# Expert results added onto token rows by GpSimd's scatter, with five result tiles, and the first expert's weights and rows loaded earlier

## The reference

```python
xn = layernorm(x)
s = attn_ref(xn, ...)         # linear attention, 16 heads, a grouped convolution over 5 rows, an MLP of 1024 with gelu
g = silu(ffn_ref(xn, ...))
return x + s * g

# ffn_ref: a small causal attention over the 4 rows of one position, then 16 experts, two for each token
ln2 = layernorm(hidden_after_attn).reshape(-1, 256)           # T = 8192 tokens
probs = softmax(ln2 @ router_weight.T)
top_p, top_i = top_k(probs, 2)
cap = 1280                                                    # slots of an expert
keep = pos < cap                                              # pos: place of the token in its expert
buf = zeros((16, cap + 1, 256)).at[exp_idx, pos_c].add(ln2[tok] * keep[:, None])
h1 = gelu(einsum('ech,efh->ecf', buf, moe_w1))                # 256 -> 512
h2 = einsum('ecf,ehf->ech', h1, moe_w2)                       # 512 -> 256
out_ent = h2[exp_idx, pos_c] * (gate * keep)[:, None]
moe_out = zeros((T, 256)).at[tok].add(out_ent)
return hidden_after_attn + moe_out
```

## Time and profile before

| | us |
|---|---|
| median of 3 runs | 2015.42 |
| lowest, highest | 2011.74, 2019.06 |
| the profiled execution | 2010.27 |
| its span, first to last instruction | 2008.5 |
| PE busy | 1806.9 (90%) |
| DVE busy | 1382.0 (69%) |
| POOL busy | 968.5 (48%) |
| ACT busy | 818.0 (41%) |

### The profile page before, as it was taken

How to read it: one execution, slowest core, us unless ns; L and a number is a source line. 1 busy time by engine, 2 the same in 40 slices (tenths; PEclk the granted TensorE clock), 3 DMA queues, 4 the chain that set the end, 5 groups by cost and what they waited for, 6 DMA issues and landing times. The chain is left out here.

```text
span 2008.5 us, 37232 instructions
## 1 busy us (share of the span) xinstructions
PE 1806.9 (90%) x12775; PEld 1616.4 (80%) x12776; DVE 1382.0 (69%) x3571; ACT 818.0 (41%) x1945; POOL 968.5 (48%) x1502
## 2 busy tenths in 40 slices
PE   3999996398999999996999999999888899999998
PEld 2676775285998858996999999999875799875998
DVE  3988885754565535653777778877567588795786
ACT  2566663262332652331333333333355333472433
POOL 3666653565555665553556656566332233340431
PEclk7999997699999999997999999999989999999999
DMA  7555522024333233333334343242136021361121
GB/s 207 160 176 177 177 93 71 27 81 129 134 126 120 71 103 112 122 123 106 112 94 127 110 134 121 92 124 71 51 121 181 22 78 58 111 192 48 53 71 59
DMA packets 181942, 218.29 MB, mean 109 GB/s; under 512 B 22874, under 2 KB 165411, under 8 KB 181774
## 3 DMA queue, kind: packets, MB, share of 16 engines
q1 hardware_dynamic: 159006, 166.61, 26.7%
q0 software_dynamic: 18464, 49.49, 7.0%
q10 hardware_dynamic: 4304, 0.02, 0.1%
HBM read 114.94 MB, written 107.22 MB: 111 GB/s over the span
## 5 line engine op out<-in xcount | busy, mean ns | idle before, releaser
L1869 POOL DMA_INDIRECT picked_d<-h,home x160 | 163.6, 1022 | 192.3 <-DVE h L1916 156.7
L1795 ACT ACTIVATE hid<-bank 128x512 f32<-128x512 f32 x160 | 95.6, 597 | 335.6 <-PE bank L130 335.6
L128 PE MATMUL bank<-rows_hi,up_hi 128*128 128x256 f32 x640 | 189.1, 295 | 11.1 <-POOL up_lo L1863 7.1
L130 PE MATMUL bank<-rows_hi,up_lo 128*128 128x256 f32 x640 | 182.5, 285 | 0.0
L129 PE MATMUL bank<-rows_lo,up_hi 128*128 128x256 f32 x640 | 182.4, 285 | 0.0
L128 PE MATMUL bank<-down_hi,hid_hi 128*128 128x256 f32 x640 | 181.2, 283 | 0.0
L130 PE MATMUL bank<-down_hi,hid_lo 128*128 128x256 f32 x640 | 181.2, 283 | 0.0
L129 PE MATMUL bank<-down_lo,hid_hi 128*128 128x256 f32 x640 | 181.1, 283 | 0.0
L1199 POOL DMA_INDIRECT buf_d<-lt,to_row x128 | 134.6, 1052 | 85.3 <-POOL lt L1195 40.7
L1498 PE MATMUL bank<-wconv,knt 128*128 128x128 f32 x1280 | 157.2, 279 | 0.0
L1930 DVE TENSOR_TENSOR hid_lo<-hid,hid_hi 128x512 fp32r<-128x512 f32 x160 | 118.8, 752 | 52.2 <-ACT hid_hi L1795 49.4
(11 more groups left out here) (318 smaller groups left out, 5587.4 us busy)
## 6 DMA issues: line engine op xcount, KB each, us to landing
buf_d<-zeros SPq DMA_DIRECT2D x16, 1360.0 KB, 7.4
rows_in<-buf_d SPq DMA_DIRECT2D x80, 272.0 KB, 2.8
lt<-ln_d SPq DMA_DIRECT2D x128, 128.0 KB, 2.2
picked_d<-nothing SPq DMA_DIRECT2D x32, 512.0 KB, 3.2
job_picked<-picked_d SPq DMA_DIRECT2D x64, 256.0 KB, 2.9
x<-in_x SPq DMA_DIRECT2D x16, 512.0 KB, 4.1
after_d<-after SPq DMA_DIRECT2D x16, 512.0 KB, 2.9
ln_d<-ln SPq DMA_DIRECT2D x16, 512.0 KB, 2.9
```

What stands on the lines that cost most here:

```text
L128: pe.matmul(dst, hi, mhi, start=start and i == 0, stop=False)
L130: mm = pe.matmul(dst, lo, mhi, start=False, stop=end)
L1795: act.activation(dst[:, 2 * half:2 * half + 2].rearrange("p f c -> p (f c)"), bank[half][:], ACT.Gelu_apprx_tanh).then_inc(e_hid, 1)
L1869: pool.indirect_dma_start(picked_d, bass.IndirectOffsetOnAxis(home[i % TAG_RING][:, r:r + 1], axis=0), h2[p][:, r], None, bounds_check=PIC ...
```

## The change

1. `send` adds: the scatter has `compute_op=ALU.add` and goes to the token's row in `after_d`, so that after the experts this row holds `hidden_after_attn` plus both expert results. The home row of both slots is the token's number (the pattern of the iota changes from `[T, 2]` to `[0, 2]`). Two experts may add to the same row, so at the first chunk of each expert POOL waits until all earlier scatters have landed. `picked_d`, its clears, `nothing`, `mix` and the load of `job_after` are gone; a job's load of `after_d` goes straight to `picked[:, 0]`, and ACT's `silu` waits for that DMA.
2. `H2_RING` goes from 3 to 5, `TAG_RING` from 6 to 9, the jobs' `RING` from 3 to 4.
3. The buffers `up_w0`, `down_w0` and `rows_in` are allocated ahead of attention A, `lt` are the first two `rows_in`. POOL asks for expert 0's weights at the start of attention A. SP asks for the first three chunks of rows at the end of attention A, after the scatters have landed.
4. Expert 0's up weights are split by ACT (high) and DVE (low), its down weights by POOL.
5. In attention B, SP asks for the fourth group of x ahead of the first job's store, and DVE does the join ahead of `stats_x`.

```diff
-PICKED = 2 * T
-        picked_d = nc.dram_tensor("picked_d", (PICKED, E), F32).ap()
-                    pool.iota(tags[:, :, :, 1], pattern=[[P, TILES], [T, 2]], base=0, channel_multiplier=1,
+                    pool.iota(tags[:, :, :, 1], pattern=[[P, TILES], [0, 2]], base=0, channel_multiplier=1,
...
-        SCATTERS, RING = TILES // 2, 3
+        SCATTERS, RING = TILES // 2, 4
+        ROWS_AHEAD, H2_RING, TAG_RING = 3, 5, 9
+        early = ExitStack()
+        up_w0, down_w0 = sb("up_w0", [P, HALVES, FFN], into=early), sb("down_w0", [P, FC, E], into=early)
+        rows_in = [sb(f"rows_in{p}", [P, 2, ROW], into=early) for p in range(ROWS_AHEAD)]
+        def load_first_weights(pool):
+            pool.dma_start(up_w0[:], a["w1_t"][0].rearrange("(j p) f -> p j f", p=P)).then_inc(weights_in[0], 16)
+            pool.dma_start(down_w0[:], a["w2_t"][0].rearrange("(j p) f -> p j f", p=P)).then_inc(weights_in[0], 16)
...
-                            sp.dma_start(picked[p][:], picked_d.rearrange("(k t p) e -> p t k e", k=2, p=P)[:, t]).then_inc(job_in[p], 16)
-                            sp.dma_start(job_after[p][:], tile(after_d, t)).then_inc(job_in[p], 16)
+                            sp.dma_start(picked[p][:, 0], tile(after_d, t)).then_inc(job_in[p], 16)
...
-                                    if 1 <= i <= CLEARS // 2:
-                                        clear_picked((b - first) * CLEARS // 2 + i - 1)
                             for q in scattered:
                                 sp.wait_ge(q, 32 * EACH)
+                            for i in range(ROWS_AHEAD):
+                                sp.dma_start(rows_in[i][:], chunk_of(buf_d, i)).then_inc(rows_loaded[i], 16)
                             for q in s_out:
                                 sp.wait_ge(q, 16 * BT)
-                            sp.wait_ge(picked_clear, 16 * CLEARS)
...
                             load_x(first, 2)
+                            load_x(first, 3)
                             for job in range(2 * EACH):
                                 store_job(job)
...
-                                if job == 0:
-                                    load_x(first, 3)
...
+                        if scatters:
+                            load_first_weights(pool)
                         flow(opening, first_loop, middle, second_loop)
...
-                            act.wait_ge(job_mixed, job + 1)
+                            act.wait_ge(job_in[job % RING], 16 * (rounds(job) + s_loads(job)))
...
-                        def mix(job):
-                            p = job % RING
-                            rows = picked[p]
-                            dve.wait_ge(job_in[p], 32 * rounds(job))
-                            dve.tensor_tensor(rows[:, 0], rows[:, 0], rows[:, 1], ALU.add).then_inc(mix_step, 1)
-                            dve.wait_ge(mix_step, job + 1)
-                            dve.tensor_tensor(rows[:, 0], rows[:, 0], job_after[p][:], ALU.add).then_inc(job_mixed, 1)
...
+                    act.wait_ge(weights_in[0], 32)
+                    act.activation(up_s[0][0][:], up_w[0][:], ACT.Copy).then_inc(first_up, 1)
...
                         if i % CHUNKS == 0:
-                            pe.wait_ge(weights_split, 4 * x + 2)
+                            if x == 0:
+                                pe.wait_ge(first_up, 2)
+                            else:
+                                pe.wait_ge(weights_split, SPLITS(x, 2))
...
                     def send(i):
                         p = i % H2_RING
                         pool.wait_ge(h2_made, i + 1)
+                        if i and i % CHUNKS == 0:
+                            for q in range(H2_RING):
+                                pool.wait_ge(h2_out[q], 32 * len(range(q, i, H2_RING)))
                         for r in range(2):
-                            pool.indirect_dma_start(picked_d, bass.IndirectOffsetOnAxis(home[i % TAG_RING][:, r:r + 1], axis=0),
-                                                    h2[p][:, r], None, bounds_check=PICKED - 1,
-                                                    oob_is_err=False).then_inc(h2_out[p], 16)
-
-                    load_weights(0)
+                            pool.indirect_dma_start(after_d, bass.IndirectOffsetOnAxis(home[i % TAG_RING][:, r:r + 1], axis=0),
+                                                    h2[p][:, r], None, bounds_check=T - 1, oob_is_err=False,
+                                                    compute_op=ALU.add).then_inc(h2_out[p], 16)
+
                     load_weights(1)
-                    for x in range(2):
-                        split_weights(x)
-                        load_weights(x + 2)
+                    pool.wait_ge(weights_in[0], 32)
+                    step = Chain(pool, weights_split)
+                    step(pool.tensor_copy(down_s[0][0][:], down_w[0][:]))
+                    step(pool.tensor_tensor(down_s[0][1][:], down_w[0][:], down_s[0][0][:], ALU.subtract))
+                    pool.wait_ge(first_up, 2)
+                    load_weights(2)
+                    split_weights(1)
+                    load_weights(3)
...
                     rows_out(0)
+                    dve.wait_ge(first_up, 1)
+                    dve.tensor_tensor(up_s[0][1][:], up_w[0][:], up_s[0][0][:], ALU.subtract).then_inc(first_up, 1)
```

60 lines of the change are left out of this document (23 added, 37 removed).

## The result

The changed kernel takes **2001.31 us** (median of 9 runs, 1996.19 to 2004.66) against 2015.42 us (median of 9, 2008.39 to 2023.54): a ratio of 0.9924, 95% interval 0.9907 to 0.9941 (the quotient of the two medians is 0.9930, inside it). The forecast was 2001.3 us, so the sum came out to the tenth. Its terms did not: the experts became 7 us longer where nothing was expected, and attention B gained some 5 us more than was summed.

A forecast was written before the change was run, and what follows sets the result against it. PE was taken as the busiest engine, with only its idle or slow stretches to win. Terms -4.6 - 1.8 + 1.5 - 4.2 - 2.0 - 3.0 = -14.1 us took 2015.42 to 2001.3 us, range 1991 to 2013.

The forecast's parts named there:

- Start of the experts, first multiplication: Experts' start: with weights and rows loaded earlier, PE's first up multiplication comes 4.6 us sooner (ends -6.1 and 0).
- The collisions after it: Experts' start: one POOL split instead of two delays chunk 2's rows, so its multiplications come 1.8 us sooner (ends 0, -3).
- The expert stage itself: Expert stage: PE stays full, and POOL has room for adding scatters of 1.0 to 1.5 us; 0 us.
- End of the experts: Experts' end: the last adding scatter lands later before the block can close, +1.5 us (between nothing and 2.8 us added).
- First batch of B: Attention B, batch one: earlier fourth x group removes a wait, -4.2 us, and the low-clock stretch after it, -2.0 us.
- The mixes: Attention B: 54 us of DVE additions go, but only the middles of the batches gain, -3.0 us (ends 0 and -4).
- POOL did not become the bound: Slower rival, experts: adding scatters over 1.85 us make POOL the bound; 2028 us at 2.04 us each; chance 0.12.
- The gains were not eaten: No-change rival: DVE held up at experts' start, no middle gains, later landing, low clock elsewhere; 2014.2 us; chance 0.14.
- The load order did help: Rival, B's batch one: the wait for the fourth x group remains, -6.2 falls away; 2007.5 us; chance 0.10.
- The range's lower end: Whole kernel: better ends of the terms (-19.3) and 3.7 us of run scatter, given as 1991 us.

The follow-up runs named there:

- e4_late: The change without its early loads: expert 0's weights and first rows asked for at the experts' start, POOL splitting both first experts; 2007.04 us, 0.9979 of before.
- e1_plain: The change with a plain scatter in place of the adding one, so a token's row holds only the last result; 1992.28 us, 0.9903 of before.
- e2_spread: The change with POOL's split of down_w, and the load behind it, two chunks later; 1988.79 us, 0.9887 of before.
- e3_xload: The kernel before with only the fourth x group asked for ahead of the first job's store; 2010.90 us, 0.9991 of before.
- e5_nomix: The kernel before without the mixes, all loads kept, experts' results left out of the output; 2009.96 us, 0.9984 of before.
- e12_spreadb: The kernel before with POOL's split of down_w and the next load two chunks later; 2012.82 us, 0.9985 of before.

## Why the prediction was right, and which of its steps were not

The total was met by luck, since errors in its terms cancel. Step by step:

*Start of the experts, first multiplication* (-4.6): **right**. From SP's last store to PE's first up multiplication 9.9 us against 14.2, -4.3; each link came within a few tenths.

*The collisions after it* (-1.8): the mechanism **right**: the second collision is gone, and the slow clock behind it; both come back in e4_late. Chunk 2's first multiplication follows chunk 0's by 12.4 us where it was 13.7, so -1.3. The forecast said 11.9, though its own terms, 9 and 2.3, make 11.3.

*The expert stage itself* (0): **wrong, and the worst of the steps**. Its price was all but inside the range (1.56 us, taken 1.0 to 1.5), its test was that an expert gives POOL 30.9 us and it uses 22.6, "so up to 0.83 us more per send is free". That asks whether POOL keeps up, and it does. It does not ask when POOL's split now falls, though the same text priced exactly this hold at the experts' start. The two sends of a chunk had grown by 1.2 us (on average, 2 x 1.62 against 2 x 1.02), which moved the split against DVE's chunk; DVE lost 5.3 us in one chunk and not 3.1, and PE lost 0.84 us in each expert with a split. +7.2 us net, +9.0 by e1_plain. e2_spread removes the overlap and leaves the price.

*End of the experts* (+1.5): landing **right** (8.67 - 7.24 = 1.4 us), but half of the term was missing: the last four sends stand in a row, each 1.85 us apart and not 1.3, so the last one starts 4.15 us after the eightieth h and not 2.74. Together +2.8. The estimate from the Trainium skill (DMA: Bandwidth & Descriptors, Latency and other measured facts), +0.2 to +2 us for the added read, holds the measured 1.4; it says nothing of POOL's own 0.56 us.

*First batch of B* (-6.2): the wait and the slow stretch went **as priced** in their stretch (-6.0 in e3_xload), though the timed runs of e3_xload leave room for no more than 4.6 us in all. But "the mixes' 0.84 us a step leave it just there, so it does not take the stall's place" was **mis-sized**: DVE, busy for 16.44 of 17 us, was already holding PE up. Without the mixes that loop is 3.2 us shorter, and in the change 8.1.

*The mixes* (-3.0, all of it in the middles): "nearly all of it is worth nothing, since PE is full beside it" was **wrong**, for the same reason: -2.3 us in batch two's first loop, where the earlier trace rows, a mean over loops and middles, hid that DVE was at 93%. The middle's -2.4 was **right in size** (-2.6), but to put the missing job loads at 0 was **wrong**: e5_nomix shows that with the loads kept nothing is gained there, as job_x takes the place of the mixes. In batch two's middle -0.6 was forecast and -1.6 measured; with the loads kept it grew by 2.1.

*The rivals.* POOL did not become the bound: 1.56 us is under the 1.85 from which it would, and DVE never waited for a landed result. The gains were not eaten. The load order did help in its stretch. But POOL did cost some 12 us below its bound, by a mechanism that the rivals had not listed.

So 2001.3 was met because errors cancelled: +8.5 us missed in and after the experts and +0.8 at their start, against 5.4 us missed in B, with the 4 us that the profiles do not assign making up the rest. (The range's lower end is added up to 1991; its terms, -19.3 and -3.7 from 2015.42, make 1992.4.) The change as made is a good one (no mixes, fewer job loads, earlier loads) with a bad one inside it (the adding scatter in front of an unspread split).

## What to carry to other kernels

A resource with time to spare can still cost time: when an operation on it becomes longer, ask not only whether its sum fits but which of its other operations are pushed, and beside what they now run. Here DVE lost 3.1 us in a chunk beside POOL or 5.3, and 0.8 us of timing that nobody had written down decided which; with the heavy operations of one put in separate chunks of the other, the sends could stay as long as they were and PE no longer waited. When work is taken off an engine, look up what feeds it as well (the loads, and their place in the queue), and split a stage into its loops before calling an engine idle: a mean over loop and middle hid one that was full.

## What the runs showed of the hardware

An indirect scatter that adds costs POOL 1.56 us for 128 rows of 1 KB where a plain one costs 1.00 (medians of 160), and moves the same bytes in more packets: 26784 in the expert stage (955 to 1465 us) against 11367 (955 to 1460 us); over the whole kernel the pages count 33824 against 18464, 96 more for each of 160 sends. It lands 4.1 us after issue and not 2.6. Only the operation differed between the change and e1_plain.

In these traces DVE operations between SBUF tiles and POOL's casts and subtractions lengthen each other. rows_lo takes up to 2.8 us for 0.69 and even a copy of 2 elements per partition 1.77 us for 0.16, beside POOL's subtraction; where hid_lo started 0.12 us ahead of POOL's cast it still took 2.28 us, and the cast 1.61 for 1.06. The Trainium skill (SBUF — State Buffer, SBUF: two separate sides) calls the port pair of the two, for a DVE operation in a two-port mode or with two SBUF inputs, an exclusive lock that whichever starts first holds for its whole instruction. The first rows agree with that (the copy ends with POOL's subtraction, rows_lo 0.55 us behind it); the last does less well, since the one that had started first was held longest.

The granted clock of a stretch without an edit differed between executions: the same 198 PE instructions in the middle of B's first batch kept PE busy for 42.5 us at 1.00 (before), 47.2 at 0.90 (e3_xload) and 45.7 at 0.94 (e12_spreadb).
